# One scan operation for each state of the selective scan, in the place of its second half

## What is computed

```python
x = in_proj_w @ ctx                    # 512 channels, 512 time steps
u = silu(conv4(x) + conv_b)
B, C, dt = parts of x_proj_w @ u       # 16 + 16 + 16 rows
delta = softplus(dt_proj_w @ dt + dt_proj_b)
A = -exp(A_log)                        # 512 channels x 16 states
state = state * exp(delta_t * A) + (delta_t * u_t) * B_t    # step over t, for each channel and state
y_t = sum over the 16 states of state * C_t
y = (y + D * u) * silu(z)
```

## Time and profile before

| Engine | busy | share of the span | instructions |
|---|---|---|---|
| TensorE (PE) | 1394.1 us | 86% | 6762 |
| VectorE (DVE) | 1110.4 us | 69% | 1547 |
| ScalarE (ACT) | 944.5 us | 58% | 2428 |
| GpSimd (POOL) | 486.6 us | 30% | 367 |

### The profile page before, as it was taken

One profiled execution on the slowest core, in us unless ns is written; L12 is line 12 of the kernel. 1 busy time (PEld: TensorE's weight loads), 2 busy tenths in 40 slices (PEclk: granted clock), 3 DMA queues, 4 the chain that ended last, 5 costly groups with the idle time before them and its releaser, 6 DMA issues.

```text
span 1619.7 us, 26021 instructions
## 1 busy us (share of the span) xinstructions
PE 1394.1 (86%) x6762; PEld 999.7 (62%) x6763; DVE 1110.4 (69%) x1547; ACT 944.5 (58%) x2428; POOL 486.6 (30%) x367
## 2 busy tenths in 40 slices
PE   4899898999999899999899999898436548999996
PEld 1577665548887455887644678763225436777774
DVE  5365598858898786878886887786853326666662
ACT  4667684468878246877725687763213325666652
POOL 0000010000143502006250210206426446666663
PEclk9799999999999999999999999999757779999998
DMA  6538987623679742576973267578124449999985
GB/s 240 201 109 223 292 204 178 151 93 81 182 193 227 179 107 80 126 230 138 226 175 94 61 173 208 116 175 250 41 87 104 102 98 222 223 238 231 243 185 67
DMA packets 137435, 265.44 MB, mean 164 GB/s; under 512 B 45944, under 2 KB 47433, under 8 KB 128512
## 3 DMA queue, kind: packets, MB, share of 16 engines
q0 software_dynamic: 36480, 126.75, 35.0%
q1 hardware_dynamic: 75120, 86.70, 18.5%
q10 hardware_dynamic: 25744, 50.87, 10.0%
HBM read 170.57 MB, written 46.21 MB: 134 GB/s over the span
## 4 chain that ended last, share of the span: by engine, by line
PE 50%; DMA 18%; issue 10%; DVE 9%; ACT 5%; SPq 3%; POOL 2%; POOLq 1%; ACTq 1%; DVEq 0%
PE bank L694 13%; PE bank L671 8%; DMA out<-y_ring,add_ids 4%; PE bank L654 4%; DMA y<-state 4%; PE pair L615 3%; PE pair L616 3%; PE pair L617 3%; DMA wout<-in_wout 2%; PE bank L532 2%; DMA c_bc<-bc_dram 2%; DMA y<-dbu 2%; PE pair L532 2%; PE pair L559 2%; DVE dbu L2103 1%
## 5 line engine op out<-in xcount | busy, mean ns | idle before, releaser
L694 PE MATMUL bank<-wout,o_t 128*128 128x512 f32 x512 | 241.0, 627 | 27.4 <-DMA wout<-in_wout 16.3
L671 PE MATMUL bank<-v_aug,probs 128*128 128x129 f32 x2048 | 249.1, 277 | 10.1 <-ACT probs L1331 7.1
L671 PEld LDWEIGHTS bank<-v_aug,probs 128*128 128x128 f32 x2048 | 240.5, 192 | 27.4 <-ACT probs L1331 19.9
L2757 POOL DMA_INDIRECT lists<-entry,slot x128 | 197.6, 1543 | 83.4 <-DVE entry L2244 44.7
L694 PEld LDWEIGHTS bank<-wout,o_t 128*128 128x128 f32 x512 | 101.2, 201 | 154.8 <-issue 154.3
L1331 ACT ACTIVATE probs<-bank 128x512 f32<-128x512 f32 x256 | 152.2, 604 | 69.0 <-PE bank L654 31.8
L1340 ACT ACTIVATE decay<-delta,neg_a 128x511 f32<-128x511 f32 x256 | 164.4, 725 | 24.4 <-DVE state L2103 12.1
L2868 POOL DMA_INDIRECT out<-y_ring,add_ids x68 | 125.0, 1838 | 96.6 <-DMA out<-y_ring,add_ids 52.3
L2772 POOL DMA_DIRECT2D y<-dbu x32 | 29.2, 913 | 412.6 <-DVE dbu L2108 254.0
L2103 DVE TENSOR_TENSOR_SCAN state<-decay,state 128x1024 f32<-128x1024 f32 x64 | 144.8, 2281 | 6.5 <-ACT decay L1340 4.7
L2103 DVE TENSOR_TENSOR_SCAN dbu<-decay,dbu 128x1024 f32<-128x1024 f32 x64 | 144.7, 2279 | 5.1 <-ACT decay L1340 4.2
(11 more groups left out here) (234 smaller groups left out, 2948.3 us busy)
## 6 DMA issues: line engine op xcount, KB each, us to landing
y<-dbu POOLq DMA_DIRECT2D x32, 1024.0 KB
wq<-wq_dram POOLq DMA_DIRECT2D x30, 1024.0 KB
y<-state POOLq DMA_DIRECT2D x28, 1024.0 KB
w_raw<-in_w_exp ACTq DMA_DIRECT2D x32, 768.0 KB
wout<-in_wout SPq DMA_DIRECT2D x64, 256.0 KB
b_bc<-bc_dram SPq DMA_DIRECT2D x64, 256.0 KB
c_bc<-bc_dram SPq DMA_DIRECT2D x64, 256.0 KB
w_raw<-in_w_exp ACTq DMA_DIRECT2D x32, 512.0 KB
```

The costliest lines, as they stand in the source:

```text
L671: mm = pe.matmul(bank_o[half][:, (t % 2) * (DH + 1):(t % 2 + 1) * (DH + 1)], probs[:, k, t * P:(t + 1) * P], v_aug[:, k, :], start=(k == 0 ...
L694: mm = pe.matmul((bank_o + bank_s)[t][:], o_t[:, h, t * P:(t + 1) * P], wout[:, h % 4, :], start=(h == 0), stop=(h == H - 1))
L2757: pool.indirect_dma_start(out=lists, out_offset=bass.IndirectOffsetOnAxis(ap=slot[:, t, k:k + 1].bitcast(U32), axis=0), in_=entry[:, t, :] ...
```

## The change

`state_scan` loses its argument `half` and is one operation over all 2048 columns. In each program the call for half 0 is gone, and the one operation stands where the call for half 1 stood. `scan_ok` counts one for each state instead of two. It waits for all four exponentials of its state, and each exponential of the next state waits for the whole of it. Nothing else moves on any engine.

```diff
@@ scan_pad (ACT), conv_start (DVE)
-                act.wait_ge(S["scan_ok"], r * DS * 2)
+                act.wait_ge(S["scan_ok"], r * DS)
...
@@ decays (ACT)
-                        act.wait_ge(S["scan_ok"], (r * DS + n - 1) * 2 + e // 2 + 1)
+                        act.wait_ge(S["scan_ok"], r * DS + n)
...
@@ state_scan (DVE)
-            def state_scan(r, n, half):
-
-                es = slice(2 * half, 2 * half + 2)
-                now = place[n % 2][:, es, :].rearrange("p e t -> p (e t)")
-                dve.wait_ge(S["dA_ok"], r * DS * ET + n * ET + 2 * half + 2)
+            def state_scan(r, n):
+
+                now = place[n % 2][:].rearrange("p e t -> p (e t)")
+                dve.wait_ge(S["dA_ok"], r * DS * ET + n * ET + ET)
                 dve.wait_ge(S["dbu_ok"], r * DS + n + 1)
-                dve.tensor_tensor_scan(now, dA3[:, es, :].rearrange("p e t -> p (e t)"), now, 0.0, ALU.mult, ALU.add).then_inc(S["scan_ok"], 1)
+                dve.tensor_tensor_scan(now, dA, now, 0.0, ALU.mult, ALU.add).then_inc(S["scan_ok"], 1)
...
@@ row(b, r) (DVE), second part of row b
                 state_input(b, 8)
                 denominators(b, 11, 0)
-                state_scan(b, 8, 0)
                 denominators(b, 11, 1)
-                state_scan(b, 8, 1)
+                state_scan(b, 8)
                 state_product(b, 8)
                 state_input(b, 9)
-                state_scan(b, 9, 0)
                 denominators(b, 12, 0)
                 q_lows(b, 3, 2)
-                state_scan(b, 9, 1)
+                state_scan(b, 9)
...
                 denominators(b, 13, 0)
                 q_lows(b, 3, 3)
-                state_scan(b, 10, 0)
                 denominators(b, 13, 1)
-                state_scan(b, 10, 1)
+                state_scan(b, 10)
                 state_product(b, 10)
                 denominators(b, 14, 0)
                 denominators(b, 14, 1)
                 first_stats(r, 0)
                 state_input(b, 11)
-                state_scan(b, 11, 0)
                 denominators(b, 15, 0)
                 first_stats(r, 1)
                 denominators(b, 15, 1)
-                state_scan(b, 11, 1)
+                state_scan(b, 11)
...
-                state_scan(b, 13, 0)
                 norm_lo(r, 1)
-                state_scan(b, 13, 1)
+                state_scan(b, 13)
...
@@ row(b, r) (DVE), first part of row r
                 denominators(r, 3, 1)
-                state_scan(r, 2, 0)
                 final_means(b)
                 final_newton(b)
                 final_norm(b, 0)
...
                 final_norm(b, 2)
-                state_scan(r, 2, 1)
+                state_scan(r, 2)
                 denominators(r, 4, 1)
                 state_product(r, 2)
                 final_norm(b, 3)
                 state_input(r, 3)
-                state_scan(r, 3, 0)
                 denominators(r, 5, 0)
                 denominators(r, 5, 1)
                 q_norm(r, "g2a")
-                state_scan(r, 3, 1)
+                state_scan(r, 3)
...
                 state_product(r, 3)
-                state_scan(r, 4, 0)
                 q_norm(r, "g2b")
-                state_scan(r, 4, 1)
+                state_scan(r, 4)
                 state_product(r, 4)
                 softmax_top(b)
...
```

More of the change, by code:

```diff
@@ L2009, in conv_start @@
                 if r > 0:
-                    dve.wait_ge(S["scan_ok"], r * DS * 2)
+                    dve.wait_ge(S["scan_ok"], r * DS)
                 link(dve.memset(x_pad[:, :, 0:DC - 1], 0.0))
@@ L2305, in first_row @@
                 state_input(0, 1)
[L2306 to L2307 removed]
+                state_scan(0, 0)
                 q_norm(0, "g1a")
[L2309 removed]
                 denominators(0, 2, 0)
@@ L2312, in first_row @@
                 state_product(0, 0)
-                state_scan(0, 1, 1)
+                state_scan(0, 1)
                 q_norm(0, "g1b")
@@ L2319, in first_row @@
                 state_input(0, 2)
-                state_scan(0, 2, 0)
                 denominators(0, 4, 0)
                 q_lows(0, 1, 3)
-                state_scan(0, 2, 1)
+                state_scan(0, 2)
                 state_input(0, 3)
@@ L2347, in row @@
                 denominators(b, 8, 0)
-                state_scan(b, 5, 0)
-                state_scan(b, 5, 1)
+                state_scan(b, 5)
                 denominators(b, 8, 1)
@@ L2354, in row @@
                 denominators(b, 9, 0)
-                state_scan(b, 6, 0)
-                state_scan(b, 6, 1)
+                state_scan(b, 6)
                 denominators(b, 9, 1)
@@ L2361, in row @@
                 denominators(b, 10, 1)
-                state_scan(b, 7, 0)
-                state_scan(b, 7, 1)
+                state_scan(b, 7)
                 state_product(b, 7)
@@ L2402, in row @@
                 first_norm(r, 1)
-                state_scan(b, 12, 0)
                 first_norm(r, 2)
                 first_norm(r, 3)
-                state_scan(b, 12, 1)
+                state_scan(b, 12)
                 norm_lo(r, 0)
@@ L2416, in row @@
                 state_input(b, 14)
-                state_scan(b, 14, 0)
-                state_scan(b, 14, 1)
+                state_scan(b, 14)
                 q_norm(r, "k")
@@ L2421, in row @@
                 state_input(b, 15)
-                state_scan(b, 15, 0)
                 q_norm(r, "q0")
-                state_scan(b, 15, 1)
+                state_scan(b, 15)
                 state_product(b, 15)
@@ L2463, in row @@
                 state_input(r, 0)
-                state_scan(r, 0, 0)
-                state_scan(r, 0, 1)
+                state_scan(r, 0)
                 denominators(r, 1, 0)
@@ L2477, in row @@
                 denominators(r, 2, 1)
-                state_scan(r, 1, 0)
-                state_scan(r, 1, 1)
+                state_scan(r, 1)
                 add_scan(b, 0)
```

11 lines of the change are left out of this document (3 added, 8 removed).

## The result

The changed kernel takes 1640.91 us (median; 1637.8 to 1645.37), the kernel before 1615.88 in the same series: ratio 1.0151, 95% interval 1.0111 to 1.0191. That is slower by more than 1%, and inside the range of 1621 to 1644, 6.4 us above the predicted 1634.5. Its profiled execution took 1637.8 us around a span of 1636.0; the one of before 1621.45 around 1619.7.

What follows compares the result with a forecast made beforehand. TensorE was taken as the bound (half of the chain of waits). Terms 1.7 + 3 x (0.4 + 2.0 + 0.9) + 3 x (0 + 0.3) + 5.0 = 17.5 us, added to the median 1616.96, gave 1634.5 us; range 1621 to 1644.

Steps and rivals of the forecast that it cites:

- The operation's price: Each scan on VectorE: one whole scan takes 4.43 us, against 4.47 for an adjoining pair of halves.
- 2.6 us of VectorE at most: All 64 states: most VectorE time saved by merging, at 0.04 us each against an adjoining pair.
- State 0: Rows 1 to 3: the next exponentials wait for the whole scan and move by 0.5; 0.4 us lost in each row.
- State 2: Rows 1 to 3: scan ends later, state 3's exponentials wait 3.3 us, softmax and scores follow; 2.0 us lost in each row.
- State 4: Rows 1 to 3: operation ends 2.15 later, ahead of the expert choice TensorE needs; 0.9 us in each row.
- Row 3: States 5 and 6 lose 1.2 us, states 9 and 10 lose 2.4 and 1.4; sum 5.0.
- Row 0: Row 0's start: state 4's operation ends 1.7 later, delaying state 3's product and the sum behind it; 1.7 us lost.
- Head 10: Row 3, states 5 and 6: all four exponentials run behind the full scan and end 1.2 us late.
- Rival 2: Rows 0 to 2, before the first projection: earlier last denominators win 6.6 us, saved operations up to 2.6; 1608; chance 0.08.
- States 8 to 15 and the projections: Rows 0 to 2: states 8 to 11 lose 2.2 and regain 2.2, sum 0; states 12 to 15 lose 0.3 each row.
- Rival 1: Throughout: slack takes up part of the loss, TensorE takes only half of each step; 1626 us; chance 0.28.
- Rival 3: GpSimd's list writes wait longer beside whole scans, delaying sums behind them; adds 13 us, 1647; chance 0.07.

Runs made afterwards that it cites:

- a2: a1 with the next state's exponentials also waiting for both halves, scans still two operations; 1642.91 us, ratio 1.0171 to the kernel before.
- a1: Kernel before with half 0 of all 38 non-adjoining pairs moved down to half 1, still two operations, waits unchanged; 1627.06 us, ratio 1.0048.
- d2: Changed kernel with state 2's scan in rows 1 to 3 as two halves, half 0 in its old place; 1636.96 us, ratio 1.0110 to the kernel before.
- a4: Kernel before with one edit: the next state's exponentials wait for both halves of the scan; 1625.27 us, ratio 1.0046.
- c1: Kernel before, unmerged: half 0 of state 1 behind product 0 (row 0), of state 11 behind the last denominators (rows 0 to 2); 1616.37 us, ratio 1.0009.
- c2: c1 with head 5's projection weights loaded ahead of head 6's, state 13's broadcasts and the next context (rows 0 to 2); 1606.88 us, ratio 0.9936.
- d3: c2 with row 3's weights of heads 10 and 11 loaded ahead of head 12's, head 10's also ahead of state 14's broadcasts; 1599.61 us, ratio 0.9891.
- d4: Kernel before with only c2's move of the load of head 5's weights, rows 0 to 2; 1615.37 us, ratio 1.0003.
- d1: Changed kernel with c2's move of the load of head 5's weights, rows 0 to 2; 1637.19 us, ratio 1.0145 to the kernel before.

## Why the prediction was right, and where it was not

**The operation's price: right.** 4.42 us against 4.43, where the adjoining pair took 4.47. The estimated 10 us of the Trainium skill (VectorE: DVE Perf Modes) aren't there: VectorE's busy time fell by 5.2 us, and a2 against the changed kernel shows no difference in the time. The measurement decides: merging an adjoining pair saves 0.05 us, because its halves overlap, and merging a scattered one 4.56 - 4.42 = 0.14. My "2.6 us of VectorE at most" was wrong by my own numbers: it took the 0.04 of an adjoining pair for all 64, where the 38 scattered ones save 0.13 each.

**State 0: right.** 0.4 forecast, 0.5 to 0.6 measured, in every trace in which the exponentials wait for both halves, and 0.0 in a1 where they don't.

**State 2: right in size, half right in its path.** 2.0 forecast, 1.78 measured three times, gone in d2. I named only ScalarE as the carrier. The larger part goes through VectorE's own order: the last step of the final norm stands behind scan and product, and TensorE's transposes wait for it (0.92 us). a1, in which the exponentials keep their head start, still has 1.2 of the 1.8.

**State 4: right.** 0.9 forecast; heads 7 to 9 brought +1.2, 0.0 and +1.5 in rows 1 to 3. Row 2's 0.0 is measured against a head 8 that comes 1.5 us sooner in a4, c1, c2, d3 and d4, which move no scan there; against these it is +1.5 too, and the term nearer 1.4 than 0.9.

**Row 3: right in the heads.** 5.0 forecast, 4.6 and 4.0 measured: 2.46 at head 14 (2.4 forecast), 1.79 less 0.35 at head 15 and the projection's start (1.4 forecast). Head 10 (1.2 forecast) isn't shown: 0.74 in one trace of the changed kernel, 0.01 in the other.

**Row 0: wrong, by 5 us.** -3.6 and -3.3 in place of +1.7. Up to head 9 it is -0.8 and -0.9. The step looked only at state 4 and the chain's one row there, and that part came: +1.3 at heads 7 and 8. It missed that half 0 of state 1 also stood ahead of product 0, so that moving it down starts the chain of sums sooner: -2.0 at head 6 (-2.4 in c1, which moves it alone in that stretch). The other -2.8 and -2.4 lie between head 9 and the projection, where I had 0: -1.7 is the shorter wait before the projection, and the 2.2 that ScalarE was to be late by ahead of it don't appear in row 0. Why they don't isn't shown. Rival 2 had the right kind of mechanism (work that comes sooner once a half is out of its way) at another place.

**States 8 to 15 and the projections: 7 us more than forecast, most of it unexplained.** "It is gone, which gives 2.2 back. Sum 0", and 0.3 for the rest. In rows 1 and 2 heads 10 to 15 brought +3.6 and +3.0, the wait before the projection shrank to 1.03 and gave 2.5 back (sum +1.6), and up to head 8 the three projections brought +0.5 for the 0.9 forecast. The other +5.5 is the stretch between heads 12 and 14, which isn't shown to be the change's. What the step did miss is what TensorE meets behind its early start (row 1): the clock's fall at head 0 went with the wait, which gave 2.9 us back, and at head 5 the weights came only 3.2 us sooner for a TensorE that was 5.3 sooner. Their load stands behind head 6's, the broadcasts of state 13 and the next context; it is issued 13.7 us after the projection's start and lands 9.5 us later. The wait grew by 2.1, and the clock fell behind it (2.6 us). I had written that the loads pace TensorE in the projection, and didn't draw this conclusion. c1 against c2 shows it: the same early start, worth nothing with the load in its place and 9.5 us with the load moved.

**The rivals.** Rival 1 (half of each step is taken up) fails: the steps in the heads came nearly in full. Rival 2 fails in its sign, as said. Rival 3's list writes came as described, 0.8 us after the scan's end and up to 5.19 us long, but by a2 they cost the changed kernel nothing that can be told; by its trace, d1 has them as the next limit, about 5 us in each of rows 1 and 2 once the weights are on time. No run has d1 without the long scans, so that reading isn't tested. The rule of the Trainium skill on which it stood (SBUF — State Buffer, SBUF: two separate sides) agrees with the traces; a rule that holds does not say that its cost is on the path.

**The total.** The sum against the profiled execution was 17.5 forecast and 17.7 measured, by errors of -5 in row 0, +7 in states 8 to 15 and the projections, and -1 in small ones, that cancel. That is luck, and the more so as 5.5 of the +7 may belong to the trace of before. The median moved by 25, 7 more than forecast, and what these 7 us are stays open. One candidate is the wait for head 11's weights in row 3, some 6 us: four of the other kernels' traces have it, and none of the changed kernel's two.

## What to carry to other kernels

Splitting an operation is worth its place, not its count: a half that fills a hole in a waiting engine costs nothing, and the same work merged at the later place costs all of it. When a change brings an engine to a stage sooner, look at what that stage is fed by before booking the gain: here the early start and the earlier load were each worth nothing that can be told, and 8 us together. And when a mask is taken away, expect the next one behind it: late weights hid a late sum. And before a difference between two traces is booked as an effect, look at the same stretch in the traces of other kernels with the same code there: here a step of 5.5 us lay in a stretch in which the trace of before is the fastest of fourteen.

## What the runs showed of the hardware that I had not expected

Two scans of 128x1024 take 4.56 us apart and 4.47 adjoining, and one of 128x2048 4.42: of the 0.14 us that a second operation costs, 0.09 are hidden when it adjoins. By the same numbers a column of the scan costs (4.42 - 2.28)/1024 = 2.09 ns, twice the 1.05 of `tensor_tensor`. A long wait of TensorE was charged twice: behind the 4.97 us at head 5 the granted clock was 0.62 and 0.70, and eight matmuls took 6.25 us in place of 3.67. In the projections of the fourteen traces the eight matmuls behind each of 46 waits of 3.04 us and more took 5.1 to 6.7 us, behind each of 68 waits of up to 2.15 us 3.67, and behind 15 between these sometimes the one and sometimes the other (3.67 behind 2.83, 5.37 behind 2.48). The same code in the same kernel met such a fall in one trace and not in another (0.50 against 0.93 in one stretch of 5 us), which alone makes projections differ by 3 us and a single trace a poor witness for steps of that size outside of the heads.
